# Layer 2 of a graph network: the two attention-logit products on separate groups of 32 output partitions

## The reference, cut to what matters

```python
x_l = (x @ W_l + b_l).reshape(n, H, C)
x_r = (x @ W_r + b_r).reshape(n, H, C)
x_j = x_l[src]
m = jax.nn.leaky_relu(x_j + x_r[tgt] + e_emb, NEG_SLOPE)      # slope 0.2
logits = jnp.einsum('ehc,hc->eh', m, att)
lmax = jax.ops.segment_max(logits, tgt, num_segments=n)
ex = jnp.exp(logits - lmax[tgt])
den = jax.ops.segment_sum(ex, tgt, num_segments=n)
alpha = ex / (den[tgt] + 1e-16)
out = jax.ops.segment_sum(alpha[..., None] * x_j, tgt, num_segments=n)
h = jax.nn.gelu(out.reshape(n, H * C) + bias, approximate=False) + x
```

## Time and profile before

| | |
|---|---|
| median of 3 runs | 3239.19 us (3236.39 to 3239.74) |
| span of the profiled execution, first to last instruction | 3236.0 us |
| PE matmul busy | 2560.1 us, 79%, 14129 records |
| DVE busy | 2647.0 us, 82% |
| ACT busy | 2099.4 us, 65% |
| POOL busy | 1871.0 us, 58% |

### The profile page before, as it was taken

The page is one execution under the profiler, slowest core; times in us unless marked ns, Lnnn a source line. Parts: engine busy times, 40 slices in busy tenths (PEclk is TensorE's granted clock), DMA queues, the critical chain, the costliest instruction groups (busy, mean ns, idle before and its releaser), DMA issues. The chain is left out here.

```text
span 3236.0 us, 46376 instructions
## 1 busy us (share of the span) xinstructions
PE 2560.1 (79%) x14129; PEld 1752.9 (54%) x14129; DVE 2647.0 (82%) x3328; ACT 2099.4 (65%) x3677; POOL 1871.0 (58%) x1771
## 2 busy tenths in 40 slices
PE   7899999959999977888888699999999752345500
PEld 3466666636666655566665456766666541234400
DVE  6599999969999987999999457888888756999910
ACT  0167776736566557999988588989989753545500
POOL 4477777523333327777775555555555006787776
PEclk9999999979999998999999899999999855666855
DMA  7357666656666656777776448878887547885211
GB/s 210 111 186 226 218 219 221 209 164 199 198 197 200 202 153 204 234 234 232 229 229 210 117 132 201 210 202 214 205 213 201 147 120 247 276 273 155 83 39 40
DMA packets 495088, 611.79 MB, mean 189 GB/s; under 512 B 66866, under 2 KB 284652, under 8 KB 494717
## 3 DMA queue, kind: packets, MB, share of 16 engines
q1 hardware_dynamic: 433030, 495.63, 50.9%
q0 software_dynamic: 56480, 111.88, 13.0%
q10 hardware_dynamic: 5334, 1.32, 0.2%
HBM read 391.94 MB, written 220.55 MB: 189 GB/s over the span
## 5 line engine op out<-in xcount | busy, mean ns | idle before, releaser
L1295 POOL DMA_INDIRECT g_xd_xs<-table_x,dst_row x196 | 200.7, 1024 | 285.1 <-PE g_psT L1363 191.1
L1817 POOL DMA_INDIRECT f_rows<-table_x,src_row x196 | 228.0, 1163 | 229.0 <-POOLq L1216 169.6
L775 POOL DMA_INDIRECT c_xs<-table_x,src_row x196 | 185.0, 944 | 303.0 <-PE c_psT L916 249.8
L765 POOL DMA_INDIRECT c_xs<-table_h,src_row x196 | 221.4, 1130 | 121.4 <-issue 78.9
L497 POOL DMA_INDIRECT xs<-in_x,src_i x196 | 227.2, 1159 | 85.4 <-issue 55.5
L482 POOL DMA_INDIRECT xd<-in_x,dst_i x196 | 216.4, 1104 | 94.8 <-issue 47.2
L1295 POOL DMA_INDIRECT g_xd_xs<-table_x,src_row x196 | 208.3, 1063 | 59.8 <-issue 59.8
L1824 POOL DMA_INDIRECT out<-f_rows,end_i x196 | 197.5, 1008 | 62.4 <-issue 62.4
L1869 PE MATMUL f_psT<-w_ident,f_rows 128*128 128x128 f32 x196 | 48.6, 394 | 220.8 <-DVE f_rows L1962 220.8
L765 POOL DMA_INDIRECT c_xd<-table_h,dst_row x196 | 185.0, 944 | 59.7 <-issue 59.7
L1368 PEld LDWEIGHTS g_psP<-w_center,g_turns 128*128 128x128 f32 x1568 | 183.7, 191 | 49.9 <-ACT g_turns L1504 28.4
(11 more groups left out here) (332 smaller groups left out, 8595.0 us busy)
## 6 DMA issues: line engine op xcount, KB each, us to landing
g_share<-shares SPq DMA_DIRECT2D x196, 192.0 KB
xn<-in_x SPq DMA_DIRECT2D x49, 512.0 KB
table_x<-xo SPq DMA_DIRECT2D x49, 512.0 KB, 2.9
table_x1b<-xb SPq DMA_DIRECT2D x49, 512.0 KB, 4.9
c_xn<-table_x SPq DMA_DIRECT2D x49, 512.0 KB
table_h<-c_xo SPq DMA_DIRECT2D x49, 512.0 KB
c_xn<-table_h SPq DMA_DIRECT2D x49, 512.0 KB
c_x1r<-table_x1b SPq DMA_DIRECT2D x49, 512.0 KB
```

Of the source, the lines that this page charges most:

```text
L765: pool.indirect_dma_start(out=quarters(rows[:, s, :])[j], out_offset=None, in_=table, in_offset=edge_index(columns, now.n, j)).then_inc(la ...
L775: pool.indirect_dma_start(out=quarters(xs[:, s, :])[j], out_offset=None, in_=table, in_offset=edge_index(h.src_row, now.n, j)).then_inc(sr ...
L1295: pool.indirect_dma_start(out=quarters(xd_xs[:, s, k, :])[j], out_offset=None, in_=table, in_offset=edge_index(columns, now.n, j)).then_in ...
L1817: pool.indirect_dma_start(out=quarters(rows[:, n, :])[j], out_offset=None, in_=table, in_offset=edge_index(h.src_row, n, j)).then_inc(src_ ...
```

## The change

The two products are no longer added up. The first has 32 weight columns and writes partitions 0 to 31 of `psA`; the second has 4 weight columns, the same ones, and writes partitions 32 to 35. Each is complete by itself. `att_s` goes, with its memset and its copy ahead of the loop. The order of instructions, all waits and signals, the copy `alike` and everything behind it stay as they are.

```diff
-        att_a, att_s = sb("att_a", [P, 36]), sb("att_s", [P, 36])
+        att_a = sb("att_a", [P, 32])
@@
-                    nc.tensor.matmul(psA[0:36, 0, :], att_a[:, :], zl[:, :], start=True, stop=False)
-                    nc.tensor.matmul(psA[0:36, 0, :], att_s[:, :], zsl[:, :], start=False, stop=True).then_inc(a_ready, 1)
+                    nc.tensor.matmul(psA[0:32, 0, :], att_a[:, :], zl[:, :], start=True, stop=True)
+                    nc.tensor.matmul(psA[32:36, 0, :], att_a[:, 0:heads], zsl[:, :], start=True, stop=True).then_inc(a_ready, 1)
@@
             nc.vector.memset(att_a[:, :], 0.0)
-            nc.vector.memset(att_s[:, :], 0.0)
@@
-            nc.vector.tensor_copy(att_a[:, 0:heads], every_head)
-            nc.vector.tensor_copy(att_s[:, 32:32 + heads], every_head).then_inc(att_ready, 1)
+            nc.vector.tensor_copy(att_a[:, 0:heads], every_head).then_inc(att_ready, 1)
```

## The result

The changed kernel takes 3208.95 us (median of 4 runs, 3207.47 to 3209.87) against 3238.35 us before (4 runs): ratio 0.991, 95% interval 0.990 to 0.992.

A forecast was written before the change was run, and what follows sets the result against it. The prediction took a ring of waits through PE, DVE and ACT, with the logit pair on it, to bound each step. 48 x 0.40 = 19.2 us off the 3236.0 us span, plus 3.2 us, gave 3220.0 us; range 3216 to 3241 us.

The forecast's parts named there:

- the overlap: On PE, the second product's first pass runs beside the first's second pass: three passes' time in place of four.
- the limit: ACT's idle before affT, 0.43 us a step, is the most a shorter logit pair can take off the step.
- The ring: A step's period runs gelu, centring, logit products, transposes, affT, second centring, DVE, ACT's layer norm, back to gelu.
- gelu's end released the first centring: On ACT, gelu's end at 2193.28 us was read as what lets PE's first centring start at 2193.40.
- The term of 0.40 us: On PE, first logit pass to transposes falls from 1.84 to 1.44 us, saving 0.40 us a step.
- 48 equal steps: Each of 48 steps with a logit pair ahead of transposes gains 0.40 us, 19.2 us in all.
- What was said to follow: The rest of the step comes earlier by 0.40 us; DVE's 1.15 us and ACT's 0.75 us waits stay.
- No overlap: Rival: the two products do not stream side by side on PE; 3239 us (3236 to 3241), chance 0.30 with exposed load.
- the slower case: Rival: PE empties before passing to other output partitions, +0.16 us a step, 3246.9 us, or +0.25, 3251.2 us; chance 0.10.
- a part of the overlap: Rival: the second product's weight loads are exposed on PE, saving 0.32 or 0.21 us, 3223.8 or 3229.1 us; chance 0.15.

The follow-up runs named there:

- e3: The kernel before with the second product over 256 of 512 columns, half the self-loop logits left out: 3218.79 us, ratio 0.994.
- e2: The kernel before without the second product, self-loop logits left out: 3211.47 us, ratio 0.991.
- e9: The changed kernel with the second product done twice, both times on partitions 32 to 35: 3237.82 us in a single run.
- e4: The changed kernel with 64 weight columns in both products, on partitions 0 to 63 and 64 to 127, all copied by alike: 3207.81 us, ratio 0.990.
- e5: The changed kernel with two more copies of the second product, on partitions 64 to 67 and 96 to 99: 3210.15 us, ratio 0.991.
- e11: The changed kernel with the first product done twice on partitions 0 to 31 before the second: 3237.76 us in a single run.
- e1: The kernel before with 32 weight columns in both products, still added up on the same partitions 0 to 31: 3238.18 us, ratio 1.000.

## Why the prediction was wrong

Two steps of its sum failed together, the overlap and the limit. Had only the overlap been wrong, the gain would have been 20.6 us; had only the limit been wrong, 19.2. Both lie inside the range.

**The ring: right in what the sum needs.** The pair was on the path that closes a step, by its place in PE's order. e3 shows it one for one (0.43 us off the pair, 15.21 to 14.78), and e2 that the shorter pair gives the whole gain of a plain step. The step adds up from three stretches of the earlier trace rows: second centring to gelu 6.94 us, gelu to `affT` 7.01, `affT` to second centring 1.26, together 15.21. In the changed kernel they are 6.94, 6.34 and 1.25, together 14.53. Only the middle one shrank. One reading in it is not shown: that gelu's end released the first centring. Gelu ends 0.11 us before that start, but the two passes of L1406 ahead of it on PE also take just 0.86 us, 0.43 each, up to it, in all kernels here; so PE's own list is not held up there. Which of the two comes last was not separated, and the pair lies behind both.

**That separate partitions let the products run side by side: right**, by e9 against the changed kernel, with e4 and e5.

**How much they overlap: wrong, the first step that failed.** The prediction put the second product's first pass "as soon as its weights are in, at 0.46 + 0.03 = 0.49", since "passes start in order". It starts at 0.01, and e11 shows that it would even go ahead of three passes standing before it. The term of 0.40 us off the pair measured 0.86 us (1.84 to 0.98), of which 0.82 reached the transposes. The case that the pair takes two passes' time was among no rivals, since I had taken order of starts for granted.

**The limit of 0.43 us: wrong, the second step that failed.** It capped the larger overlap at 48 x 0.43 = 20.6 us. The idle of 0.43 us before `affT` is not what ACT can give. ACT's records overlap when it does not wait: in the changed kernel `values` starts 1.00 us before `alike` though its record is 1.11 long, and `alike` starts 0.48 us before `affT` though its record is 0.59. In the earlier trace rows, `alike` was 0.59 long and ended at 2198.75, so `affT` could have started at 2198.64. `alike` itself started 1.12 us behind `values`, whose row is missing there:

```profile
2197.04 1.10 ACT L1524 ACTIVATE g_values<-g_psZ,cols 128x1024 f32<-128x1024 f32 x1
```

Its pace is 1.00, so 0.12 us of waiting was hidden in the overlap. 0.43 + 0.11 + 0.12 = 0.66 us, against 0.68 measured per plain step. The 6.34 us from gelu's start to `affT`'s are ACT's unbroken run.

**48 equal steps: wrong in the other direction.** In the changed kernel one full step in seven stays at 16.4 us. There DVE works without a hole through the maximum between chunks, the exponents and `pre2` (15.26 us busy in 16.40), and it did so before (15.27 in 16.41), without the wait of 1.15 us ahead of `pre2`: the pair was not on that step's path. 48 x 0.68 would be 32.6 us; 27.0 were gained between the first and the last L1533. So 0.68 us in place of 0.40 per plain step is the miss, and the unequal steps hid a part of it.

**What was said to follow.** ACT's wait for the sums stayed (0.75, now 0.76). DVE's wait for the second centring did not: 1.15 became 0.68 us. DVE's work ahead of it begins with `pre1`, which ACT's scalings release and which starts 4.09 us behind gelu in both kernels; the centring came 0.68 us earlier behind gelu, that work, with a small hole in it closed, only 0.21. DMA and POOL took the shorter step without a new wait of weight: POOL's wait for the transposes of gathered rows is the cover, 167.2 us in place of 191.1. Weight widths, memset and copy cost nothing, as said.

**The rivals.** No overlap and the slower case are refuted by the starts in the trace; a part of the overlap too. The Trainium skill, "TensorE: Matmul & The Clock Gate", Part 3, has the load rule (loads overlap matmuls in flight only in another row group). The changed kernel contradicts it as the earlier trace rows did: second-pass weights load at 2194.46 and 2194.48 while passes on the same 128 input partitions run until 2194.90.

**Still open.** It is not shown by what means a product overtakes the ones before it.

## What to carry to other kernels

Small products with few weight columns that stand next to each other on PE should go to separate groups of 32 or 64 output partitions, each complete by itself. Up to four then cost what one does (e5 against e2), and padding them to add up costs the full time of each. What stands behind them gains only until the next thing it waits for, here `nodeT`. One signal, on the last of them in the program, is enough (e11). Before giving such a saving a cap, take the pace of the following engine from starts, not from ends and idle: records overlap by a tenth of a microsecond each. And ask which steps have an extra user of the same bank before a copy out of it is delayed.

## What the runs showed of the hardware

- Float32 products of 512 columns on separate groups of output partitions start 0.01 us apart and run at full speed side by side: two, or four, take 0.98 us to the next full-array work where nothing else holds it, against 1.84 us for two on the same partitions (changed kernel, e5; e1). I had expected a shared read path or one pass of delay. The Trainium skill, "TensorEngine Tiling (Array Packing)", Key Properties, says that different tiles operate in parallel, and the trace agrees.
- Matmuls do not start in program order across groups (e11): a product started 0.44 us ahead of a pass that stands before it. The Trainium skill, "TensorE: Matmul & The Clock Gate", Part 3, says that matmuls start and end in program order; for the starts, that holds here within a group only (e9). The signal of the overtaking product still came last, 0.92 us behind the end of its own record (e11).
- Groups of 64 partitions gave the same as groups of 32 (e4: 1.01 us where `nodeT` does not hold the transposes), and each product of them may have all 64 weight columns.
- The granted clock fell to 0.54 in a stretch of 3.5 us behind an idle of 2.62 us on PE in the changed kernel, and not behind the same idle in the kernel before (1.00). It cost 1.49 us in one centring (3.54 against 2.05 us).
